# Gated linear attention and a split-precision FFN on one core: x also loaded transposed, normalisation shifts on GpSimd, branch bodies exchanged, new instruction orders

## The reference

```
q, k, v = x@Wq, x@Wk, x@Wv;  fg = sigmoid(x@Wf + bf)      # 16 heads of 8
state_t = state_{t-1} * fg_t + v_t (outer) k_t              # 8x8 per head, along the sequence
o_t     = state_t q_t
att = (norm(o) * gamma + beta) * silu(x@Wg) @ Wout
x1  = norm(x + att)
h   = silu(x1@w1*s1) * (x1@w2*s2)                            # 128 -> 512
h   = gelu(h@h1*sh1);  h = gelu(h@h2*sh2)                    # 512 -> 512, twice
out = norm(x1 + h@w3*s3)                                     # 512 -> 128
```

## Time and profile before

| | us |
|---|---|
| median of 3 runs | 583.79 |
| lowest and highest of them | 579.83, 586.04 |
| the profiled execution | 584.93 |
| span of its trace, first to last instruction | 582.5 |

### The profile page before, as it was taken

The page is one execution under the profiler, slowest core; times in us unless marked ns, Lnnn a source line. Parts: engine busy times, 40 slices in busy tenths (PEclk is TensorE's granted clock), DMA queues, the critical chain, the costliest instruction groups (busy, mean ns, idle before and its releaser), DMA issues.

```text
span 582.5 us, 7709 instructions
## 1 busy us (share of the span) xinstructions
PE 520.5 (89%) x2536; PEld 391.6 (67%) x2536; DVE 497.1 (85%) x871; ACT 395.1 (68%) x685; POOL 241.1 (41%) x239
## 2 busy tenths in 40 slices
PE   4546289999999999999999999999999999888994
PEld 1114157868787777778786878777777778666863
DVE  0397599999999999999999999999999999894311
ACT  2552157777777777777787777777777778676753
POOL 0900045152534445453616253544545362535460
PEclk9667689999999999999999999999999999899998
DMA  7899909476684929392948668593929297000001
GB/s 287 204 247 238 230 5 236 107 181 162 154 208 115 248 71 251 78 257 68 254 109 204 157 166 196 137 224 86 257 73 266 58 252 170 0 20 0 19 0 37
DMA packets 32056, 87.82 MB, mean 151 GB/s; under 512 B 2320, under 2 KB 18960, under 8 KB 23568
## 3 DMA queue, kind: packets, MB, share of 16 engines
q1 hardware_dynamic: 32016, 87.31, 60.7%
HBM read 74.72 MB, written 12.58 MB: 150 GB/s over the span
## 4 chain that ended last, share of the span: by engine, by line
DVE 59%; PE 19%; issue 8%; ACT 5%; POOL 4%; DMA 3%; SPq 0%; POOLq 0%; ACTq 0%
DVE KJ L449 15%; DVE QJ L460 12%; PE F L737 7%; DVE QJ L466 6%; DVE h L511 6%; DVE stats L470 4%; ACT o_norm L302 3%; DVE KJ L439 3%; DVE shift_o L491 3%; PE back L678 3%; POOL rstd_o L225 3%; DVE stats_o L470 2%; DMA KJ<-qk_bounce 2%; PE back L625 2%; PE F L711 2%
## 5 line engine op out<-in xcount | busy, mean ns | idle before, releaser
L216 POOL TENSOR_TENSOR h1lo<-h,h1hi 128x512 fp32r<-128x512 f32 x64 | 89.8, 1416 | 186.5 <-ACT h1hi L337 186.5
L216 POOL TENSOR_TENSOR h2lo<-h,h2hi 128x512 fp32r<-128x512 f32 x64 | 81.2, 1290 | 73.3 <-ACT h2hi L337 73.3
L344 ACT ACTIVATE h<-F,cols 128x512 f32<-128x512 f32 x128 | 86.4, 686 | 17.7 <-PE F L737 17.3
L439 DVE TENSOR_TENSOR KJ<-ps_v,KJ 128x1024 f32<-128x1024 f32 x64 | 77.0, 1205 | 18.6 <-DMA KJ<-qk_bounce 18.6
L711 PE MATMUL F<-h1hi,whi 128*128 128x512 f32 x256 | 80.4, 448 | 0.9 <-DVE h L511 0.7
L711 PE MATMUL F<-h2hi,whi 128*128 128x512 f32 x256 | 78.0, 438 | 0.9 <-ACT h L344 0.9
L449 DVE TENSOR_TENSOR_SCAN KJ<-g,carry,KJ 128x512 f32<-128x512 f32 x64 | 78.7, 1262 | 0.0
L460 DVE TENSOR_TENSOR QJ<-QJ,KJ 128x1024 f32<-128x1024 f32 x64 | 76.0, 1210 | 0.0
L449 DVE TENSOR_TENSOR_SCAN KJ<-g,KJ 128x512 f32<-128x512 f32 x64 | 74.7, 1201 | 0.0
L737 PE MATMUL F<-h1lo,whi 128*128 128x512 f32 x256 | 68.8, 412 | 0.0
L741 PEld LDWEIGHTS back<-w,h 128*128 128x128 f32 x512 | 61.9, 191 | 3.3 <-DVE x1lo L507 0.3
(11 more groups left out here) (77 smaller groups left out, 816.6 us busy)
## 6 DMA issues: line engine op xcount, KB each, us to landing
KJ<-qk_bounce SPq DMA_DIRECT2D x32, 1024.0 KB, 12.6
QJ<-qk_bounce SPq DMA_DIRECT2D x32, 1024.0 KB, 8.3
qk_bounce<-qk SPq DMA_DIRECT2D x32, 256.0 KB, 7.3
x_in<-in_x SPq DMA_DIRECT2D x16, 256.0 KB, 8.9
out<-res SPq DMA_DIRECT2D x16, 256.0 KB, 7.7
h<-in_wffn SPq DMA_DIRECT2D x2, 1024.0 KB, 8.3
res<-in_wffn SPq DMA_DIRECT2D x2, 256.0 KB, 4.5
wproj<-in_wproj SPq DMA_DIRECT2D x1, 384.0 KB, 3.5
```

The costliest lines, as they stand in the source:

```text
L216: e.tensor_tensor(h_lo[layer][:, t, :], h[:, t, :], h_hi[layer][:, t, :].bitcast(f32), ALU.subtract).then_inc(lo_done[layer], 1)
L344: e.activation(dst[:, t, :], F[t][:], ACT.Gelu, scale=scale[t]).then_inc(gelu_done[layer], 1)
L439: e.tensor_tensor(K, vb, K, ALU.mult).then_inc(kv_done, 1)
```

## The change

- The host also passes x with the tokens along the free dimension (`in_xT`, 16 blocks of 128 x 512). SyncE loads it into two buffers `xT[0]`, `xT[1]` (`load_xT`). `transpose_x` and `copy_xT` are gone; the projections wait for the DMA. `x_in` is now read by `residual_1` alone.
- `rstd_of` on GpSimd also computes the shift, by two more instructions on 128 x 4 elements; `shift_of` on VectorE is gone.
- The `If` tests for zero: the body without wlo products stands directly behind the branch. The branch stands later in the program, inside step 2.
- The orders on all five engines are new. ScalarE, VectorE and SyncE now work on tile s where they worked on s-1.

```diff
+            def load_xT(n):
+                if n >= 2:
+                    e.wait_ge(gate_made, n - 1)
+                e.dma_start(xT[n % 2][:], xT_d[n]).then_inc(xT_landed[n % 2], 16)
...
-            for s in range(NB + 6):
-                n = s - 2
-                if live(n):
-                    fetch(n, 1, 0)
+            for s in range(NB + 5):
+                n = s
+                if live(n):
+                    if n > 1:
+                        load_xT(n)
+                n = s - 1
+                if live(n):
                     send(n, 0)
                     fetch(n, 1, 1)
                     fetch(n, 0, 0)
-                n = s - 1
+                n = s
                 if live(n):
                     send(n, 1)
-                n = s - 2
+                n = s - 1
                 if live(n):
                     fetch(n, 0, 1)
-                n = s - 6
+                n = s - 5
                 if live(n):
                     store(n)
                 n = s
                 if live(n):
-                    if n > 1:
-                        load_x(n)
+                    fetch(n, 1, 0)
+                n = s - 1
+                if live(n):
+                    load_x(n)
...
                 e.tensor_tensor(rstd[k][:], mv[k][:, :, 1], eps4[:], ALU.add).then_inc(ve_done[k], 1)
+                e.tensor_tensor(shift[k][:], mv[k][:, :, 0], minus4[:], ALU.mult)
                 e.wait_ge(ve_done[k], n + 1)
                 e.tensor_tensor(rstd[k][:], rstd[k][:], mhalf4[:], ALU.pow).then_inc(rstd_done[k], 1)
+                e.wait_ge(rstd_done[k], n + 1)
+                e.tensor_tensor(shift[k][:], shift[k][:], rstd[k][:], ALU.mult).then_inc(shift_done[k], 1)
...
-            def copy_xT(n):
-                e.wait_ge(xT_made, n + 1)
-                if n:
-                    e.wait_ge(gate_made, n)
-                e.activation(xT[:], front[:], ACT.Copy).then_inc(xT_copied, 1)
...
-            def shift_of(n, k):
-                e.wait_ge(rstd_done[k], n + 1)
-                e.scalar_tensor_tensor(shift[k][:], mv[k][:, :, 0], -1.0, rstd[k][:], ALU.mult, ALU.mult).then_inc(shift_done[k], 1)
...
             def project_k(n):
-                e.wait_ge(xT_copied, n + 1)
-                freed((xT_copied, n), (gate_done, n - 1), (tanh_done, n - 1), (q_copied, n - 1), (k_copied, n - 1))
-                e.matmul(front[:], WK, xT[:], start=True, stop=True).then_inc(k_made, 1)
+                e.wait_ge(xT_landed[n % 2], landed(n))
+                freed((gate_done, n - 1), (tanh_done, n - 1), (q_copied, n - 1), (k_copied, n - 1))
+                e.matmul(front[:], WK, xT[n % 2][:], start=True, stop=True).then_inc(k_made, 1)
...
-            with e.If(n_low != 0):
-                for s in range(FIRST_UP, NB + 4):
-                    step(s, True)
-            with e.Else():
-                for s in range(FIRST_UP, NB + 4):
+            with e.If(n_low == 0):
+                step(FIRST_UP, False, first=False)
+                for s in range(FIRST_UP + 1, NB + 4):
                     step(s, False)
+            with e.Else():
+                step(FIRST_UP, True, first=False)
+                for s in range(FIRST_UP + 1, NB + 4):
+                    step(s, True)
```

More of the change, by code:

```diff
@@ L59, in build_program @@
         x_in = [sb(f"x_in{p}", [P, NC_ * D]) for p in range(XB)]
-        xT = sb("xT", [P, T])
+        xT = [sb(f"xT{p}", [P, T]) for p in range(2)]
         qk = sb("qk", [P, 2, T])
@@ L247, in _ @@
                     lo(2, n, 3)
-                n = s - 3
+                n = s - 1
+                if live(n):
+                    rstd_of(n, "1")
+                    lo(1, n, 0)
+                    lo(1, n, 1)
+                    lo(1, n, 2)
+                    lo(1, n, 3)
+                n = s
+                if live(n):
+                    rstd_of(n, "o")
+                n = s - 2
                 if live(n):
@@ L604, in _ @@
                 if live(n):
-                    add(n, 0)
                     add(n, 1)
+                n = s
+                if live(n):
+                    kv(n, 0)
                 n = s - 3
@@ L609, in _ @@
                     residual_2(n)
+                n = s - 2
+                if live(n):
+                    hmul(n, 2)
+                n = s - 1
+                if live(n):
+                    save_carry(n)
+                n = s - 2
+                if live(n):
+                    hmul(n, 3)
                 n = s
                 if live(n):
-                    kv(n, 0)
+                    kv(n, 1)
+                n = s - 1
+                if n == 0:
+                    find_low_parts()
+                if live(n):
+                    stats_o(n)
+                n = s
+                if live(n):
+                    scan(n, 0)
+                n = s - 3
+                if live(n):
+                    stats_2(n)
+                n = s
+                if live(n):
+                    scan(n, 1)
+                    scan(n, 2)
+                    scan(n, 3)
+                    kv(n, 2)
+                n = s - 1
+                if live(n):
+                    gated_y(n)
+                n = s
+                if live(n):
+                    kv(n, 3)
+                    scan(n, 4)
+                n = s - 1
+                if live(n):
+                    residual_1(n)
+                if n == 0:
+                    set_flag()
+                if live(n):
+                    stats_1(n)
+                n = s
+                if live(n):
+                    scan(n, 5)
+                    scan(n, 6)
+                    scan(n, 7)
+                    qs(n, 0)
+                    qs(n, 1)
+                n = s - 1
+                if live(n):
+                    x1_lo(n)
+                n = s
+                if live(n):
+                    qs(n, 2)
         @block.tensor
@@ L643, in project_f @@
+                freed((k_copied, n), (gate_done, n - 1), (tanh_done, n - 1), (q_copied, n - 1))
+                e.matmul(front[:], WQ, xT[n % 2][:], start=True, stop=True).then_inc(q_made, 1)
             def project_f(n):
[L644 to L646 removed]
+                e.wait_ge(xT_landed[n % 2], landed(n))
@@ L861, in _ @@
             for s in range(FIRST_UP):
                 step(s, False)
+            step(FIRST_UP, False, second=False)
             e.wait_ge(w3_scaled, 1)
```

443 lines of the change are left out of this document (192 added, 251 removed).

## The result

The changed kernel takes **663.3 us** (median of 4 runs, 661.47 to 664.48) against 583.8 of the kernel before: ratio **1.137** [1.130, 1.1435], slower. The prediction said 565 us, range 557 to 580, and faster. Its sign was wrong.

A forecast was written before the change was run, and what follows sets the result against it. VectorE was taken to bound the kernel at 31.46 us a step, with TensorE nearly full and next at 30.8. 584.9 less 11.2 (steps), 6.4 (fill) and 2.1 (last step) gave 565 us, range 557 to 580.

The forecast's parts named there:

- that of Q over SyncE: Ring through VectorE, GpSimd, ScalarE and SyncE's fetch of Q's second half: 29.9 us, below TensorE's 30.8, so not the bound.
- the slower one (602 us): Rival: Q's second half lands after 10.7 us behind a full queue, loop 33.2 us, total 602; chance 0.07.
- The step: Each middle step falls from 31.46 to 30.6 us; 13 steps gain 11.2 us, bounds 0 and 20.
- TensorE's bound of 30.8: Shortest step TensorE allows: 31.42 us less 0.27 recorded idle and 0.35 for the transposes of x.
- The fill: Time until the second tile is normalised: stall behind the branch goes, 6.4 us gained, bounds 0 and 10.7.
- The last step: Step before the last normalisation o: 30.6 us instead of 32.73, 2.1 us gained, bounds 0 and 4.4.
- VectorE's shifts: Three shifts leave VectorE: 1.8 us of a step, leaving it 29.1 us.
- The Q loop: Rival: the fetch of Q's second half takes 9.0 us, loop 31.5, steps gain nothing, total 578.5; chance 0.12.
- The moved jump: Rival: the jump now ends the body that runs, behind the last product; total 565 or 568 us; chance 0.07.
- the kept stall: Rival: TensorE's stall behind the branch stays, being the flag's load; the fill gains nothing, total 571.6; chance 0.11.
- The start: Start of the kernel: first k goes out about 1.3 us earlier, but its fetch meets the weight loads; cost at nothing.

The follow-up runs named there:

- e1: The changed kernel with two buffers each for rstd and shift of normalisation 2, nothing else: 558.0 us, ratio 0.953 to the kernel before.
- e2: The changed kernel with normalisation 2 moved on ScalarE from behind the copy of k to ahead of normalisation o: 556.3 us, ratio 0.950 to the kernel before.
- e11: The changed kernel with normalisation 2 moved later on ScalarE, from ahead of the copy of q to behind it: 696.6 us.
- e12: The changed kernel with normalisation 2 moved on ScalarE ahead of the last gelu, two high parts and the copy of k: 639.9 us.
- e3: e1 with SyncE also fetching Q's second half ahead of the send of the next tile's k: 556.1 us, ratio 0.950 to the kernel before.
- e6: The kernel before, in its old order, with only the shifts moved from VectorE to GpSimd: 567.8 us, ratio 0.971.
- e5: The kernel before with only the two branch bodies exchanged: 577.8 us, ratio 0.988.
- e7: The kernel before with only x also loaded transposed, without transpose_x and copy_xT, orders as before: 583.1 us, ratio 0.998.

## Why the prediction was wrong

**The step that failed** is the sentence "GpSimd gains 1.2 us of small work a step, with 14.0 of 31.4 us busy: only its part in the loop counts." It prices GpSimd by durations. What its instructions wait for, and what is queued behind the waiting one, was not asked, although the new order put `rstd_2`, with a wait on ScalarE, ahead of the four low parts, and TensorE's low products behind these. The runs showed in its place a wait of 10.2 us on GpSimd in a step; the low parts end 8.2 us later for it, and the step is 37.9 us with the wait and 30.3 without it (e1), where I had 30.6. The forecast walked one ring, that of Q over SyncE, and the true ring shares only its GpSimd and ScalarE pieces. The ScalarE order shown ahead of the prediction has `res` behind the high parts and the copy of k. With GpSimd's order, which stands in the kernel alone, the ring could be seen from that row. The excerpt was used for the copy of k, and nothing was made of the row under it. None of the rivals held this wait, the slower one (602 us) included. e1, e2, e11 and e12 show it by taking it away in two ways and moving it in two directions.

**What held and what didn't, seen where the wait is gone (e3, if no other is named):**
- *The step.* I said 30.6, near TensorE's bound of 30.8; it is 30.16, and TensorE is full (60.34 of 60.34 us). The bound was too high: in e6 TensorE keeps the transposes of x and takes 30.5, where my accounting had 31.15. The recorded idle time and the transposes' 0.35 us were not all that it could give up; what the rest is, no run shows.
- *The fill.* I said 6.4 us; it was 8.3 there (80.33 instead of 88.63) and 8.6 in the changed kernel. The transpose of x1 comes at 64.0 in the changed kernel (64.34 in e3) instead of 72.12, said 64.3. The changed kernel:

```profile
64.00 0.66 PE L644 MATMUL back<-ident,x 128*128 128x128 f32 x4 [3.72 <-ACT x L320]
```

- *The last step.* I said 2.1; it is 29.06 instead of 32.73, 3.7. Of that, 1.3 is luck with the clock: e5 and e7 take 31.40 and 31.41 there at a granted clock of 1.00, where the kernel before has 0.95. That leaves 2.3, close to what I said.
- *VectorE's shifts.* I gave 1.8 us of a step, hidden behind TensorE except for 0.9 with the transposes' part. e6 has 0.94 from the shifts alone, 31.46 to 30.52 from tile 1 to 14: the size is right, the bound behind it is not, as said above.
- *The Q loop.* Real, and seen to bind in one step of the changed kernel (31.1) and one of e1 (31.4), with landings of 9.0 and 9.2 us.
- *The moved jump and the kept stall.* In e5 tile 1 comes 7.2 us earlier and the end 7.0. From the last product to the end it is 8.2 us in both kernels, so the jump costs nothing at the end, as said. That the stall would stay is refuted.
- *xT.* On its own it leaves the step at 31.4 in e7, where VectorE is the bound. Of its 1.8 us, 0.8 come from the fill and 1.3 from the last step, which is as short in e5 without xT. So xT alone is hardly worth anything. The start, which I cost at nothing, is 2.0 us later in e7 (53.47 instead of 51.48 for tile 0).

The change with nothing but the wait taken away is e1: 558.0 us, 7 under the forecast and at the lower end of the range. With the wait, the forecast was 98 us off.

## What to carry to other kernels

In a pipeline with in-order engines, a new order is checked wait by wait, those that guard a buffer against being overwritten too: for each instruction moved ahead of others, ask which earlier tile's reader it waits for, where that reader now stands on its own engine, and what is queued behind the wait. A wait that cost nothing in the old order is no evidence for the new one; second buffers of 128 x 4 numbers, one for rstd and one for shift, were worth 105 us here. When a part of a change is measured alone, it has that price only in that order: the branch was worth 7.0 us and then nothing, the shifts 17.0 and then 6.0.

## What the runs showed of the hardware

- **Collisions of VectorE and GpSimd depend on what meets.** Two products QJ x KJ beside low parts took 4.45 us instead of 2.33, and four low parts 6.89 instead of 5.03. With no low part beside them, two products took 2.33 us in e1 too, so it isn't DMA, which is as busy there. A scan that reads g and KJ beside such low parts was not slowed. In e1 (VectorE's timeline) it starts at 300.12, with the low parts running from 298.70 to 303.73 at 1.26 us each:

```profile
300.12 1.27 DVE L482 TENSOR_TENSOR_SCAN KJ<-g,carry,KJ 128x512 f32<-128x512 f32 x1
```

  The Trainium skill (GPSIMD Engine Reference, Specifications) has contention for VectorE instructions with two SBUF inputs. By that rule the products agree and this scan does not; why is open.
- **A wait costs TensorE its clock as well.** Behind 5.7 us in which it was busy 1.8, the granted clock was 0.50 and then 0.69, and 1.00 from 315.00 on; nine products took 3.77 us, 419 ns each instead of 232. In the changed kernel this adds little to a step all the same, at most 0.5 us, because normalisation 1 is ready at almost the same time.
